# Softmax stage of a four-layer graph network: the running maximum of one group placed between another group's statistics and their scale on VectorE, and the exponentials ahead of the normalizations on ScalarE

## The reference

```python
alpha = (q[dst] * k[src]).sum(-1) * (1.0 / np.sqrt(C))
m = jax.ops.segment_max(alpha, dst, num_segments=n)
a = jnp.exp(alpha - m[dst])
denom = jax.ops.segment_sum(a, dst, num_segments=n)
agg = jax.ops.segment_sum(a[:, :, None] * v[src], dst, num_segments=n)
agg = agg / jnp.maximum(denom, 1e-16)[:, :, None]
out = agg.reshape(n, HEADS * C) + (x @ Wskip + bskip)
...
x = _layernorm(x + _L2_gnn_ref(...), axis=-1)
x = _layernorm(x + _L3_gnn_ref(x, edge_weight, src, dst), axis=-1)
```

## Time and profile before

| | |
|---|---|
| median of three runs | 7573.66 us (7573.18 to 7587.37) |
| profiled execution, device time | 7579.2 us |
| span of its trace | 7577.1 us, mean granted TensorE clock 0.843 |
| VectorE busy | 4566.0 us, 60% of the span |
| TensorE busy | 4996.8 us, 66% |
| GpSimd busy | 4815.5 us, 64% |
| ScalarE busy | 2745.5 us, 36% |

### The profile page before, as it was taken

How to read it: one execution, slowest core, us unless ns; L and a number is a source line. 1 busy time by engine, 2 the same in 40 slices (tenths; PEclk the granted TensorE clock), 3 DMA queues, 4 the chain that set the end, 5 groups by cost and what they waited for, 6 DMA issues and landing times.

```text
span 7577.1 us, 104573 instructions
## 1 busy us (share of the span) xinstructions
PE 4996.8 (66%) x26540; PEld 3423.6 (45%) x26540; DVE 4566.0 (60%) x8424; ACT 2745.5 (36%) x5600; POOL 4815.5 (64%) x4823
## 2 busy tenths in 40 slices
PE   0088799997777799999888988777777611111111
PEld 0055566665555677777644444444444311010100
DVE  8855577776666688888533333588888732222222
ACT  0044455554444344444322222377777500000000
POOL 0054566644656576666477777577777677777777
PEclk9999999999999899999899999888888755555555
DMA  0022466666999798888655555433333322222221
GB/s 15 13 82 84 116 196 195 196 197 170 217 224 219 209 257 252 252 250 251 173 155 148 150 154 155 118 108 107 109 109 107 85 65 66 65 66 65 66 65 57
DMA packets 871313, 1058.31 MB, mean 140 GB/s; under 512 B 144418, under 2 KB 505776, under 8 KB 871078
## 3 DMA queue, kind: packets, MB, share of 16 engines
q1 hardware_dynamic: 717578, 805.42, 34.4%
q0 software_dynamic: 153600, 251.49, 16.2%
HBM read 613.72 MB, written 454.66 MB: 141 GB/s over the span
## 4 chain that ended last, share of the span: by engine, by line
DVE 26%; PE 24%; issue 16%; POOL 16%; ACT 7%; DMA 6%; DVEq 5%; SPq 1%; ACTq 0%; POOLq 0%
PE bank L942 10%; POOL gat L645 7%; PE bank L844 5%; POOL xT L645 5%; DVE x L1661 4%; POOL out_rows L658 4%; PE bank L928 3%; DVE ln3vr L1649 2%; DVE t L1722 2%; ACT mbuf L1085 2%; PE bank L931 2%; DMA Z2E<-zE 2%; DMA gat<-X,d_x 2%; PE bank L930 2%; DVEq L1838 2%
## 5 line engine op out<-in xcount | busy, mean ns | idle before, releaser
L844 PE MATMUL bank<-ident,gat 128*128 128x128 f32 x2400 | 452.4, 319 | 1476.1 <-DVE zT L1690 1370.3
L1085 ACT ACTIVATE mbuf<-t 128x512 f32<-128x512 f32 x500 | 315.7, 631 | 2094.3 <-DVE t L1902 1351.9
L844 PEld LDWEIGHTS bank<-ident,gat 128*128 128x128 f32 x2400 | 311.8, 165 | 1633.2 <-issue 1285.3
L942 PE MATMUL bank<-W2s,hT 128*128 128x128 f32 x6400 | 875.7, 293 | 0.0
L1671 DVE TENSOR_TENSOR gat<-gat,pays 128x512 f32<-128x512 f32 x400 | 273.0, 682 | 993.4 <-DMA gat<-X,pays 955.2
L942 PEld LDWEIGHTS bank<-W2s,hT 128*128 128x128 f32 x6400 | 796.6, 203 | 94.5 <-issue 94.5
L928 PE MATMUL bank<-x1T,W1x 128*128 128x512 f32 x1600 | 803.5, 615 | 25.1 <-ACT x1T L1077 16.2
L671 POOL DMA_INDIRECT pays<-PAY,s_q x400 | 379.4, 948 | 626.2 <-DMA PAY<-payl 338.0
L844 PE MATMUL bank<-ident,x 128*128 128x128 f32 x3200 | 512.0, 284 | 236.1 <-DVE x L1661 231.3
L645 POOL DMA_INDIRECT gat<-in_x_rows,pays x400 | 395.0, 987 | 369.7 <-PE bank L844 264.9
L1141 ACT ACTIVATE hT<-bank,b1u 128x512 f32<-128x512 f32 x800 | 506.6, 687 | 256.8 <-PE bank L931 251.8
(11 more groups left out here) (342 smaller groups left out, 11849.2 us busy)
## 6 DMA issues: line engine op xcount, KB each, us to landing
X<-x SPq DMA_DIRECT2D x700, 256.0 KB, 3.9
fB<-row_s_same SPq DMA_DIRECT2D x400, 256.0 KB, 5.3
xT<-in_x_fm SPq DMA_DIRECT2D x200, 256.0 KB
out_rows<-x SPq DMA_DIRECT2D x200, 256.0 KB
ffB<-rows_last_notlast SPq DMA_DIRECT2D x100, 512.0 KB
Z1T<-zT SPq DMA_DIRECT2D x100, 256.0 KB, 2.1
Z1E<-zE SPq DMA_DIRECT2D x100, 256.0 KB
Z2T<-zT SPq DMA_DIRECT2D x100, 256.0 KB, 10.0
```

What stands on the lines that cost most here:

```text
L844: mm = pe.transpose(dst[:, t, :], tiles[t], ident[:, :])
L942: mm = pe.matmul(bMLP[:, t, :], hT[h][s][:, t * P:(t + 1) * P], W2s[:, h, :], start=False, stop=h == HC - 1, skip_group_check=True)
L1085: act.activation(sq[k % 3][s % 2], [bT1, t2[s], bSK, t2[s]][k][:, :, :], ACT.Square).then_inc(S(f"squared{k}", s), 1)
```

## The change

ScalarE takes `att_exp` of g-1 ahead of the two norms of g-4 instead of behind them. VectorE takes `att_max` of g-1 ahead of `scale34` of g-4. No instruction is added or taken away, no buffer, semaphore or lag changes. Lines behind L1195 are one higher in the changed kernel.

```diff
@@ -1192,8 +1192,9 @@
             all_slots(act, "st_x3_", EI * 16)
             all_slots(act, "mlp", NI + 2 * EI)
             all_slots(act, "mm1", NI + EI)
-            steps(act, EI, (att_src, 0), (att_q, 0), (norm(2, x3, lambda i, s: reuse(act, "st_x3_", s, EI + i, 16)), 4),
-                  (norm(3, x4, lambda i, s: reuse(act, "scattered2", s, i, 64)), 4), (att_exp, 1), (std34, 3))
+            steps(act, EI, (att_src, 0), (att_q, 0), (att_exp, 1),
+                  (norm(2, x3, lambda i, s: reuse(act, "st_x3_", s, EI + i, 16)), 4),
+                  (norm(3, x4, lambda i, s: reuse(act, "scattered2", s, i, 64)), 4), (std34, 3))
@@ -1882,7 +1883,7 @@
-            steps(dve, EI, (scale34, 4), (att_max, 1), (att_weigh, 2), (att_scores, 0), (att_sum, 2), (att_out, 3))
+            steps(dve, EI, (att_max, 1), (scale34, 4), (att_weigh, 2), (att_scores, 0), (att_sum, 2), (att_out, 3))
```

## The result

The change takes **7499.5 us** (median of 4 runs, 7494.3 to 7508.2) against 7573.4 us of the kernel before (4 runs, 7565.8 to 7587.4) beside it: ratio 0.9903, 95% interval 0.989 to 0.9916. The profiled execution took 7508.2 us, span 7506.2.

The account below looks back on a forecast made before the run. VectorE was taken to set the softmax stage's 11.63 us period, stalling ahead of the reciprocals. Gain 65.5 us minus 6 given back is 59.5; 7573.7 - 59.5 = 7514 us, range 7500 to 7539.

Parts of the forecast that it names:

- ScalarE at **0: Softmax stage: ScalarE's later exponentials and norms cost 0, covered by the slack ahead of its square roots.
- Two table loads a step stay two: ScalarE, softmax stage: still two table loads in each slot step, each 1.283 us in the mean.
- The split of ScalarE's idle time: Softmax stage: idle splits into about 0.4 to 1.7 us ahead of exponentials and 0.7 to 1.9 ahead of square roots.
- Nothing queues: SyncE's queue: the x3 store waits for the first norm but does not hold the next x2d load; cost 0.
- 97 x 66.2 / 98 = 65.5 us gained: VectorE, softmax stage: the stall ahead of the reciprocals goes in 97 of the slot steps, 65.5 us gained.
- What is given back: VectorE's own queue work in the new order: 0.06 us a step, 6 us; at worst 29 us.
- Until now the branch was covered by the stall: VectorE, step opening an iteration: the stall ahead of the reciprocals hid the loop's branch, which the change uncovers.
- Rival 4: VectorE: gaps vanish with the stall, 70 to 76 us gain, about 7500 us; chance 0.10.
- Rival 1: VectorE: the stall turns into queue work of 0.3 us or more, 36 us gain, 7537 us; chance 0.10.
- Rival 2: GpSimd becomes the bound: issues grow 5%, period 11.27 us, gain 35 us, 7539 us; chance 0.07.
- Rival 3: VectorE's scan waits for the scores, everything behind it late: 78 us slower, 7651 us; chance 0.04.
- The table switch: ScalarE: skill's 1.38 us drain per switch gives 11.1 us a step, 10 us less gain; left out.

Follow-up runs that it names:

- e2_act_only: Kernel before with only ScalarE's new order (exponentials ahead of the norms), VectorE's order kept: 7574.6 us, ratio 0.9997.
- e10_unrolled_dve_only: Kernel before with VectorE's new order, its softmax-stage list written out without a loop, ScalarE's order kept: 7462.7 us, ratio 0.9856.
- e3b_unrolled: The changed kernel with VectorE's softmax-stage list written out without a loop: 7458.5 us, ratio 0.9862 to the kernel before.
- e9_before_unrolled: Kernel before with VectorE's softmax-stage list written out without a loop: 7542.4 us, ratio 0.9961.
- e5_lag5: Kernel before, both engines' orders kept, with scale34 and the two norms five groups back instead of four: 7577.0 us, ratio 1.0002.
- e6b_lag5_scatter7: Kernel before with scale34 and norms five groups back instead of four, GpSimd's scatters seven instead of six: 7548.1 us, ratio 0.9988.

## Why the prediction was right or wrong

**Right: which wait goes, and that nothing takes its place.** The idle time ahead of the reciprocals was to be near 2 us (1.7 in 3 times over the whole stage; the stretch above, which ends at 5943, has one of them), that ahead of the scan below 20 (14.8). ScalarE at **0**: e2_act_only shows 0.9997, and e10_unrolled_dve_only shows the same with 0.33 us a step less room. "Two table loads a step stay two": 98 and 98, 1283 ns each, as in the earlier trace rows. The split of ScalarE's idle time was named with 0.4 to 1.7 us ahead of the exponentials (measured 0.9 a step) and 0.7 to 1.9 ahead of the square roots (1.7). GpSimd was to wait 0.3 us a step for ScalarE; it waits 0.6. The stage behind did not change. The places in the step came out close (T is the end of the statistics): in the step at 5396.19 the reciprocals start at T + 3.1 us (forecast 3.3) and the norms end at T + 7.4 (7.8), in the opening step at T + 9.5 (9.0). "Nothing queues" was off for SyncE: its queue now waits 441.4 us for the norms in the stage (165.7 before), and TensorE's L1030 waits 86.4 us for loads (55.0 before). The cost of it was still 0, since the scan waits 3.2 us for the scores (2.9 before).

**Wrong: the price of the stall, "97 x 66.2 / 98 = 65.5 us gained".** The term took the idle time in brackets for the whole cost. The measured step is (5440.08 - 5396.49) / 4 = 10.90 us against 11.63, so 0.73 where 0.61 was forecast; between the scans 70.8 us went where the sum had 59.5. That is 11.3 of the 14.5 us that the forecast missed by, and the other 3.2 are inside the spread of the medians.

The starts in four steps of either timeline show of what it is made, against 0.29 us behind the statistics and 0.08 behind the scale where nothing stands between (e3b_unrolled), which is 4 x 0.37 = 1.48 for four steps. Before: from the statistics to the reciprocals 1.09, 1.08, 0.93 and 1.15 us, from the last L1868 to the scan 0.26, 0.28, 0.16 and 0.35. Together 5.30, that is 3.82 too much. With the change: from the statistics to the scan 0.89, 0.38, 0.30 and 0.29, from the last L1869 to L1823 0.15, 0.16, 0.08 and 0.17. Together 2.42, that is 0.94 too much. The difference is 2.88, or 0.72 a step. The four steps stand for the stage: summed from its first scan to its last, the same distances are 102.4 and 25.3 us before, 44.4 and 13.7 with the change, which is 69.6 of the 70.8 us.

By parts, a step gains 0.68 us of idle time and 0.09 of overlap lost at the reciprocals, it gains 0.12 of the 0.18 that stood ahead of the scan, and it loses 0.18 behind the statistics, nearly all at the opening: 0.68 + 0.09 + 0.12 - 0.18 = 0.71. The 0.09, 8.7 us in 97 steps, has no term in the prediction, though the text ahead of it says that neighbouring rows overlap by about 0.1 us. The queue's own work gives back 0.18 - 0.12 = 0.06 a step, the 6 us of "What is given back". That it fits is luck: the term was half of a gap of 0.11, and the two parts that it is really made of, 0.18 and 0.12, are both larger. Seen from the whole, nothing of the 65.5 was given back, and about 5 us more were won (70.8 - 65.5). Of the 11.3 us, the 8.7 are explained; the last 2.6 the rows do not split further.

The opening did grow, from 0.19 to 0.50 us of idle time once in four steps, and the prediction was right to name it. Its sentence "Until now the branch was covered by the stall" fell with e9_before_unrolled: writing out the loop is worth 25.9 us with the stall and 26.2 without.

**The rivals.** Rival 4, gaps vanish with the stall, 70 to 76 us and about 7500, is what happened (70.8 us between the scans, 7499.5); it had a chance of 0.10, and the range stopped at 7500, inside it. Its reason was only half named: the gap, but not the overlap. The rows had a sign of it, since in the earlier trace rows the scan starts 0.16 us behind an instruction of 0.15, without overlap, while ScalarE's second norm in the earlier trace rows starts 0.10 before the first has ended. Rival 1 would have left 0.3 us a step as issue time; the 0.50 at the opening is 0.12 a step. Its sign was real, though: the 0.19 us from the square roots to the reciprocal are 0.03 without the register wait. Rival 2, GpSimd as the bound: its step goes at 10.57 in e3b_unrolled with scatters of 1.015 and gathers of 1.026 us, under the 10.73 that I computed, since the scatters got shorter (1.085 before), by more than the gathers got longer (0.997 before). Rival 3, the scan behind the scores: 3.2 us in all in the change. It is real, though, and close: e5_lag5 and e6b_lag5_scatter7 both fell into it, and gave back all of the stall and most of it.

**The table switch.** The drain of about 1.38 us a switch that the Trainium skill states ("ScalarE: Activation LUTs", "What ACT_TABLE_LOAD costs") would have made ScalarE's step 11.1 us by the prediction's estimate. In e10_unrolled_dve_only a step is 10.57 us, and ScalarE fits both switches into it and waits 188.1 us in 91 times for the scale besides, 2.1 us each; 11.1 us of work would not fit. The measurement decides.

## What to carry to other kernels

Price an in-order engine's stall by the distance between the starts of its neighbours, with and without the wait, not by the idle time in brackets: here, without loops, 0.55 us of idle was a cost of 0.72, and of the loop's 26 us only 16 (11.6 + 4.8) showed as idle. Cover a round trip to another engine with work that the queue holds anyway; moving the consumer back by a whole group does it too, but then every queue behind it (here GpSimd's scatters and SyncE's store) has to move with it, or the wait returns at the next instruction. And where a loop of an engine that sets the pace opens with a gap, as here behind a drain and a short instruction, try its opening behind a long one, or write the loop out. All of this was worth its price on undisturbed chips only.

## What was not expected of the hardware

- VectorE starts an instruction about 0.08 us before the one ahead of it has ended (0.29 us behind the start of statistics that take 0.38). It loses this overlap at a wait for ScalarE, and also where a wait on a register's value stands: 0.38 us behind the statistics in the loop's second step, where the order of instructions shows one, against 0.30 and 0.29 in the next two.
- A wait on a register's value costs VectorE about 0.16 us behind the release (stall 0.71 us against 0.55 with a constant; 0.19 behind ScalarE's last square root against 0.03), so this stall of half a microsecond did not hide it. The whole loop, the opening's branch included, costs 26.2 us in the stage, 0.27 us a step of 10.9.
- ScalarE's table load runs ahead of the wait for the exponentials' input in most steps, and behind it in about a fourth. In the groups of the change's stage VectorE's zin ends 51.5 us of idle time ahead of the load and 35.5 ahead of the activation: in 23 steps the load itself waited, 2.2 us each, and in 75 the load was done ahead and the activation waited 0.5 us in the mean.
